# A graph block's last part: batch-normalised columns by graph or by node, and who issues the stores

## The reference

```python
x = layernorm(x + attention(x, bias=adj + adj))        # 16 heads, per graph
top1 = argmax(x.mean(nodes) @ router_w + router_b)      # one of 4 experts per graph
out = adj @ (x @ expert_w[top1])
mean, var = moments of out over all nodes of all graphs of the same expert, per feature
y = relu((out - mean[top1]) * rsqrt(var[top1] + eps) * gamma[top1] + beta[top1])
x = layernorm(x + y)
```

## Time and profile before

| what | us |
|---|---|
| runs: median (lowest to highest) | 3041.95 (3036.92 to 3044.52) |
| profiled execution, its own time | 3046.38 |
| its span, first to last instruction | 3044.6 |
| PE busy / DVE busy / ACT busy / POOL busy | 2802.0 / 2191.3 / 1772.6 / 750.3 |
| first instruction of `phase_two` on SP | 2713.8 |
| first scaling of the last part | 2735.4 |
| last final ends | 3039.94 |

### The profile page before, as it was taken

One profiled execution on the slowest core, in us unless ns is written; L12 is line 12 of the kernel. 1 busy time (PEld: TensorE's weight loads), 2 busy tenths in 40 slices (PEclk: granted clock), 3 DMA queues, 4 the chain that ended last, 5 costly groups with the idle time before them and its releaser, 6 DMA issues. The chain is left out here.

```text
span 3044.6 us, 70536 instructions
## 1 busy us (share of the span) xinstructions
PE 2802.0 (92%) x24130; PEld 2369.6 (78%) x24130; DVE 2191.3 (72%) x3938; ACT 1772.6 (58%) x6146; POOL 750.3 (25%) x431
## 2 busy tenths in 40 slices
PE   6899999999999999999999999999999999766675
PEld 6788888888888888888888888888888888655554
DVE  7777777777777777777777777777777777628776
ACT  3555655555565555556556555655655555517777
POOL 2022222222222222222222222222222222121111
PEclk9999999999999999999999999999999999867666
DMA  6344444444444444444444444444444444477887
GB/s 224 117 162 173 155 145 172 167 146 162 172 150 150 172 160 146 169 172 145 156 172 159 145 172 166 144 162 172 154 149 172 160 144 162 156 268 265 331 329 267
DMA packets 165115, 537.82 MB, mean 177 GB/s; under 512 B 15539, under 2 KB 48307, under 8 KB 122035
## 3 DMA queue, kind: packets, MB, share of 16 engines
q1 hardware_dynamic: 165042, 536.96, 49.4%
HBM read 427.84 MB, written 109.05 MB: 176 GB/s over the span
## 5 line engine op out<-in xcount | busy, mean ns | idle before, releaser
L548 ACT ACTIVATE prob<-prob,neg_max 128x128 f32<-128x128 f32 x2048 | 795.3, 394 | 361.9 <-DVE abs_max L675 361.9
L323 POOL TENSOR_TENSOR norm<-norm,constants 128x1 f32<-128x1 f32 x128 | 70.8, 553 | 1621.0 <-DVE norm L707 1621.0
L525 ACT ACTIVATE qk<-bank 128x512 f32<-128x512 f32 x256 | 153.1, 599 | 466.1 <-PE bank L343 466.1
L616 DVE SCALAR_TENSOR_TENSOR prob<-bank,adj_in 128x512 f32<-128x512 f32 x512 | 318.0, 684 | 137.0 <-PE bank L343 137.0
L548 ACT ACTIVATION_READ_ACCUMULATOR prob<-prob,neg_max 128x1 f32 x2048 | 394.1, 192 | 0.0
L334 POOL TENSOR_TENSOR moments<-moments,conv 128x1024 f32 x128 | 309.0, 2414 | 328.4 <-ACT conv L573 317.5
L633 DVE TENSOR_TENSOR prob<-prob,inv_sum 128x2048 f32<-128x2048 f32 x128 | 338.8, 2647 | 4.4
L343 PE MATMUL bank<-xT_hi,wq_hi 128*128 128x256 f32 x1024 | 303.4, 296 | 39.9 <-DVE wk_lo L587 19.1
L649 DVE TENSOR_REDUCE neg_max<-prob 128x16 f32<-128x2048 f32 x128 | 291.0, 2274 | 0.0
L343 PE MATMUL bank<-xT_hi,wq_lo 128*128 128x256 f32 x1024 | 290.1, 283 | 0.0
L343 PE MATMUL bank<-xT_lo,wq_hi 128*128 128x256 f32 x1024 | 290.1, 283 | 0.0
(11 more groups left out here) (111 smaller groups left out, 6465.2 us busy)
## 6 DMA issues: line engine op xcount, KB each, us to landing
expert_hi<-expert_hi_scratch SPq DMA_DIRECT2D x128, 1024.0 KB, 4.8
expert_lo<-expert_lo_scratch SPq DMA_DIRECT2D x128, 1024.0 KB, 7.5
xT_in<-xT SPq DMA_DIRECT2D x64, 512.0 KB, 8.5
x_in<-x SPq DMA_DIRECT2D x128, 256.0 KB, 7.9
x_scratch<-x SPq DMA_DIRECT2D x128, 256.0 KB, 8.3
conv_scratch<-conv SPq DMA_DIRECT2D x128, 256.0 KB, 8.4
conv_in<-conv_scratch SPq DMA_DIRECT2D x32, 1024.0 KB, 7.1
x_in<-x_scratch SPq DMA_DIRECT2D x32, 1024.0 KB, 9.1
```

The lines of the kernel that those rows point to most:

```text
L525: act.activation(qk[:, npar, c, :, :].rearrange("p k n -> p (k n)"), src[:, :], ACT.Copy).then_inc(qk_copied, 1)
L548: last = act.activation(prob[:, u % 2, h, :], prob[:, u % 2, h, :], ACT.Exp, bias=neg_max2[:, u % 2, h:h + 1], scale=2.0, accum_out=row_su ...
L616: dve.scalar_tensor_tensor(out=prob[:, u % 2, h:HEADS:HPC, :], in0=ps_heads[h][:, :].rearrange("p (c m) -> p c m", c=C), scalar=HALF_SCALE ...
```

## The change

The two scratch tensors are laid out (graph, node, feature). In the last part a partition holds four neighbouring nodes of one graph: partition b * 32 + i has nodes 4i to 4i + 3 of graph b of the group, so that loads and stores are contiguous runs of 8 KB on both sides, where the stores were four runs of 2 KB per partition. The slot's four rows (j) are now the four nodes of a partition. A turned 128 x 128 block therefore holds columns of all four graphs, in the order (b, i), and one feature chunk c of one j. PE gathers in a bank the four j of one chunk; a scaling instruction takes one chunk and one graph: four runs of 32 columns, 128 apart. ACT scales chunks 0, 1, 2, DVE chunk 3, so both need the experts of all four graphs of the group and read them at the head of the group. `bnT` gets two buffers of a whole group.

The step of the pipeline becomes one group instead of one graph, on PE, ACT and DVE. PE turns group g and then turns back g - 1; ACT scales g and finishes g - 2; DVE scales its chunk of g, makes the shift of g - 2 and joins g - 1. The store is issued by ACT, behind its four finals and a wait for them, and SP only loads, as soon as the slot's earlier store has landed.

```diff
-    x1_dram = nc.dram_tensor("x1_scratch", (P, B, D), F32, kind="Internal").ap()
+    x1_dram = nc.dram_tensor("x1_scratch", (B, N, D), F32, kind="Internal").ap()
...
-    conv_dram = nc.dram_tensor("conv_scratch", (P, B, D), F32, kind="Internal").ap()
+    conv_dram = nc.dram_tensor("conv_scratch", (B, N, D), F32, kind="Internal").ap()
...
+    def by_token(t, lo, n):
+        return t[bass.ds(lo, n), :, :].rearrange("b (i j) d -> (b i) (j d)", j=G)
+    def flat(t, r):
+        return t[:, r, :, :].rearrange("p j d -> p (j d)")
+    def per_graph(ps, b):
+        return ps[:, :].rearrange("p (j b i) -> p j b i", j=G, b=G)[:, :, b, :]
...
-                sp.dma_start(conv_in[:, r, :, :], conv_dram[:, bass.ds(g * G, G), :]).then_inc(ld_g[r], 16)
...
-            if live(g - STORE_LAG):
-                b, r2 = g - STORE_LAG, (r - STORE_LAG) % RING
-                sp.wait_ge(finished, (b + 1) * G)
-                sp.dma_start(out[bass.ds(b * G, G), :, :].rearrange("b n d -> n b d"),
-                             x1_in[:, r2, :, :]).then_inc(st_g[r2], 16)
+                sp.dma_start(flat(conv_in, r), by_token(conv_dram, g * G, G)).then_inc(ld_g[r], 16)
+                sp.dma_start(flat(x1_in, r), by_token(x1_dram, g * G, G)).then_inc(ld_g[r], 16)
```

On PE:

```diff
+        def group(k, r, live):
+            g = k * RING + r
+            if live(g):
+                pe.wait_ge(ld_g[r], (k + 1) * 32)
                 for c in range(C):
+                    if live(g - 1):
+                        if c < ACT_CHUNKS:
+                            pe.wait_ge(act_scaled, (g - 1) * ACT_CHUNKS + c + 1)
+                        else:
+                            pe.wait_ge(dve_scaled, (g - 1) * (C - ACT_CHUNKS) + c - ACT_CHUNKS + 1)
+                    for j in range(G):
+                        last = pe.transpose(ps_turned[c][:, j * P:(j + 1) * P],
+                                            conv_in[:, r, j, c * P:(c + 1) * P], ident[:, :])
+                    last.then_inc(turned, 1)
+            h = g - 1
+            if live(h):
+                pe.wait_ge(act_scaled, h * ACT_CHUNKS + ACT_CHUNKS)
+                pe.wait_ge(dve_scaled, h * (C - ACT_CHUNKS) + C - ACT_CHUNKS)
+                for j in range(G):
+                    if live(h - 1):
+                        pe.wait_ge(joined, (h - 1) * G + j + 1)
+                    for c in range(C):
+                        last = pe.transpose(ps_back[j][:, c * P:(c + 1) * P],
+                                            bnT[:, (r - 1) % 2, c, j, :, :].rearrange("p b i -> p (b i)"),
+                                            ident[:, :])
+                    last.then_inc(turned_back, 1)
```

On ACT:

```diff
+        def group(k, r, live):
+            g = k * RING + r
+            if live(g):
+                es = [act.value_load(expert_of[0:1, bass.ds(g * G + b, 1)], min_val=0, max_val=E - 1)
+                      for b in range(G)]
+                if live(g - 2):
+                    act.wait_ge(turned_back, (g - 1) * G)
+                for c in range(ACT_CHUNKS):
+                    act.wait_ge(turned, g * C + c + 1)
+                    for b in range(G):
+                        column = bass.ds(es[b] * C + c, 1)
+                        last = act.activation(bnT[:, r % 2, c, :, b, :], per_graph(ps_turned[c], b), ACT.Identity,
+                                              bias=shift_t[:, column], scale=scale_t[:, column])
+                    last.then_inc(act_scaled, 1)
+            h, r3 = g - 2, (r - 2) % RING
+            if live(h):
+                act.wait_ge(shift_made, h + 1)
+                for j in range(G):
+                    act.activation(x1_in[:, r3, j, :], x1_in[:, r3, j, :], ACT.Identity,
+                                   bias=shift[:, r3 % 4, j:j + 1],
+                                   scale=rstd[:, r3 % 4, j:j + 1]).then_inc(finished, 1)
+                act.wait_ge(finished, (h + 1) * G)
+                act.dma_start(by_token(out, h * G, G), flat(x1_in, r3)).then_inc(st_g[r3], 16)
```

On DVE:

```diff
+        def group(k, r, live):
+            g = k * RING + r
+            if live(g):
+                es = [dve.value_load(expert_of[0:1, bass.ds(g * G + b, 1)], min_val=0, max_val=E - 1)
+                      for b in range(G)]
+                if live(g - 2):
+                    dve.wait_ge(turned_back, (g - 1) * G)
+                for c in range(ACT_CHUNKS, C):
+                    dve.wait_ge(turned, g * C + c + 1)
+                    for b in range(G):
+                        column = bass.ds(es[b] * C + c, 1)
+                        last = dve.tensor_scalar(bnT[:, r % 2, c, :, b, :], per_graph(ps_turned[c], b),
+                                                 scale_t[:, column], shift_t[:, column], ALU.mult, ALU.add)
+                    last.then_inc(dve_scaled, 1)
+            if live(g - 2):
+                finish_stats(g - 2, (r - 2) % RING, live)
+            h, r1 = g - 1, (r - 1) % RING
+            if live(h):
+                join(h, r1, 0)
+                join(h, r1, 1)
+                take_stats(h, r1, 0)
+                join(h, r1, 2)
+                take_stats(h, r1, 1)
+                join(h, r1, 3)
+                take_stats(h, r1, 2)
+                take_stats(h, r1, 3)
+                dve.wait_ge(stats_taken, (h + 1) * G)
...
+                    last = dve.bn_aggr(mean_var[:, r1 % 2, j, :], stats[:, j, :])
...
```

More of the change, by code:

```diff
@@ L758, in phase_two @@
     x1_in = sb("x1_in", [P, RING, G, D])
-    bnT = sb("bnT", [P, G, C, P])
+    bnT = sb("bnT", [P, 2, C, G, G, ROWS])
     stats = sb("stats2", [P, G, 6])
@@ L787, in phase_two @@
     finished = sem("finished")
[L789 to L797, removed]
     def run_groups(eng, group, lag):
@@ L857, in _ @@
         pe.wait_ge(columns_ready, 1)
[L859 to L865, removed]
-                for c in range(C):
[L867 to L877, removed]
@@ L881, in _ @@
+        run_groups(pe, group, 1)
     @block.gpsimd
@@ L899, in _ @@
         act.wait_ge(columns_ready, 1)
[L901 to L918, removed]
@@ L922, in _ @@
+        run_groups(act, group, 2)
     @block.vector
@@ L964, in finish_stats @@
                                      in1=rstd[:, r % 4, :], op0=ALU.mult, op1=ALU.mult).then_inc(shift_made, 1)
[L966 to L984, removed]
-                dve.bn_stats(stats[:, j, :], x1_in[:, r, j, :]).then_inc(stats_taken, 1)
-                if j == G - 1:
-                    dve.wait_ge(stats_taken, m + 1)
-                    dve.sem_inc(dve_passed)
-                    for i in range(G):
-                        last = dve.bn_aggr(mean_var[:, r % 2, i, :], stats[:, i, :])
-                    last.then_inc(stats_joined, 1)
-                    dve.wait_ge(stats_joined, g + 1)
-                    dve.tensor_scalar(var_eps[:, r % 2, :], mean_var[:, r % 2, :, 1], EPS, None,
-                                      ALU.add).then_inc(var_ready, 1)
-            m, (r, j) = n - JOIN_LAG - 2, place(s, JOIN_LAG + 2)
-            if live(m) and j == G - 1:
-                finish_stats(k * RING + (s - JOIN_LAG - 2) // G, r, live)
@@ L999, in _, with join, take_stats @@
-        run_graphs(dve, graph, JOIN_LAG + 2)
+        def join(h, r, j):
+            dve.wait_ge(turned_back, h * G + j + 1)
+            dve.scalar_tensor_tensor(out=x1_in[:, r, j, :], in0=ps_back[j][:, :], scalar=0.0,
+                                     in1=x1_in[:, r, j, :], op0=ALU.max, op1=ALU.add).then_inc(joined, 1)
+        def take_stats(h, r, j):
+            dve.wait_ge(joined, h * G + j + 1)
+            dve.bn_stats(stats[:, j, :], x1_in[:, r, j, :]).then_inc(stats_taken, 1)
+        def group(k, r, live):
[25 more added lines that the diff above has]
+                dve.wait_ge(stats_taken, (h + 1) * G)
+                dve.sem_inc(dve_passed)
+                for j in range(G):
+                    last = dve.bn_aggr(mean_var[:, r1 % 2, j, :], stats[:, j, :])
+                last.then_inc(stats_joined, 1)
+                dve.wait_ge(stats_joined, h + 1)
+                dve.tensor_scalar(var_eps[:, r1 % 2, :], mean_var[:, r1 % 2, :, 1], EPS, None,
+                                  ALU.add).then_inc(var_ready, 1)
@@ L1002 @@
+        run_groups(dve, group, 2)
 def kernel(x, adj, L0_gnn_Wq, L0_gnn_Wk, L0_gnn_Wv, L0_gnn_Wo, L1_gnn_router_w, L1_gnn_router_b,
```

24 lines of the change are left out of this document (6 added, 18 removed).

## The result

The changed kernel takes 3107.23 us at the median of four runs (3106.27 to 3108.85), the kernel before 3040.76: ratio 1.0216, 95% interval 1.0204 to 1.0228. The forecast was 3070 in 3040 to 3102. The direction was right, the size was not: +66 us instead of +28. The profiled execution took 3108.85 us, its span 3107.0.

A forecast was written before the change was run, and what follows sets the result against it. The prediction took ACT's in-order queue to bound the last part: 10.2 us a group against 9.3, with fill, loops' ends and tail +27 to +28 us, added to the median 3041.95 for 3070 us, range 3040 to 3102.

The forecast's parts named there:

- What bounds the kernel before: Last part: ACT in order, 9.3 us a group, 7.08 of it work, 2.3 reads and waits for TensorE; transfers hidden.
- ACT, work: 12 scalings and 4 finals per group stay at 7.08 us; scalings in runs of 32 add 0.
- ACT, reads: Four expert reads at each group's head, none hidden, 0.6 us each, 2.4 in all; ends 0.38 and 1.0 a read.
- The rule of the Trainium skill: Floor near 600 ns for a tensor_load: four reads some 1.3 us dearer, stage about 40 us longer; set aside for 286 ns.
- ACT, store: Per group on ACT: wait for its own finals 0.03 us and store issue 0.6, ends 0.1 and 1.2.
- DVE 10.0 us, just under ACT: DVE's work and four reads per group sum to 10.0 us against ACT's 10.2, so it doesn't set the period.
- DMA: worth nothing: Stores going from 2 KB to 8 KB runs gain nothing, as a group asks for 308 GB/s, less than today's 333.
- Fill, loops, tail: Last part: round 3 starts at 25.3 us, three loops' ends add 4.7, the tail stays 16.4.
- The sum: Last part: last group's scaling starts 315.6 us after the first, against 288.2 before; total +27 to +28 us.
- Reads cheaper: Rival at each group's head: below 0.38 us a read the change wins, 3002 us with reads quite hidden; chance 0.08.
- ACT and DVE catch each other: Rival: both near 10 us a group, or short runs dearer, +0.8 a group, 3093 us; chance 0.16.
- The DMA rival: DMA engines are the real bound in the last part and 8 KB stores free them, 3010 us; chance 0.04.

The follow-up runs named there:

- b2: Kernel before, its store cut to the first 128 bytes of every row: 3015.85 us, ratio 0.9916 to the kernel before.
- e7: Changed kernel, its store cut to the first 512 bytes of every partition, order, waits and issues untouched: 3072.76 us, ratio 1.0101 to the kernel before.
- e2: Changed kernel with the store issued by SP again, four groups behind its loads; ACT neither waits nor issues: 3101.42 us, ratio 1.0191.
- e8: Changed kernel with the store on SP and the last part's loop written out, DVE's reads still at its group's head: 3087.80 us, ratio 1.0143.
- e6: Changed kernel with store on SP in 2 KB runs, no loop, ACT scaling all four chunks: 3014.63 us, beside 3013.21 us with 8 KB runs.
- e10: e4 with the wait for the finals and the store back on ACT: 3088.90 us, ratio 1.0151 to the kernel before.
- e3: Changed kernel with the three passes of the last part's loop written out, nothing else changed: 3090.35 us, ratio 1.0153 to the kernel before.
- e4: e8 with DVE reading the next group's experts one by one between its statistics and joins: 2988.34 us, ratio 0.9818 to the kernel before.
- e9: e4 with the store in four runs of 2 KB per partition, as in the kernel before: 2992.63 us, ratio 0.9833 to the kernel before.
- e1: Changed kernel with ACT's wait for finals and store issue moved behind its four expert reads: 3086.51 us, ratio 1.0140 to the kernel before.

## Why the prediction was wrong

The mechanism was right as far as it went: ACT's reads stand exposed behind its own wait and store, and ACT bounds the stage. The profile shows the signs that were named, one idle stretch a group put down to issue, scalings 0.34 apart, no wait for a load. The size of one term was not right, since two reads of a group are slowed by the store.

*What bounds the kernel before.* Right in naming ACT's in-order queue and in calling the transfers hidden. It took the 2.3 us of idle time for reads and waits for TensorE; b2 shows that about 0.9 of it was the collision.

*ACT, work: 7.08 us, runs of 32 at no charge.* Right: 7.10, scalings 0.34 apart.

*ACT, reads: four at 0.6, 2.4 us.* This is the step that failed. Measured 3.5: two of the four run beside the packets of the store that ACT has just issued, and are slow. The store and the reads were both in the sum, but priced one by one. The step had the warning in front of it, a load of 1683 ns, and put the end of its range at 1.0 us a read without asking which reads were long. Load by load, the trace of before shows it: from the fourth group on, the first and third read of a group take 0.27 to 0.30 us (one 0.37, and the first behind a branch 0.97 and 0.98), the second 0.65 to 1.71 in every group; the stores begin just there. The second read of the group of the earlier trace rows:

```profile
L907 ACTq TENSOR_LOAD <-expert_of x1: 1027/1027/1027, 2862.1 to 2862.1; - x1
```

By e7 against the changed kernel this is 35 of the 38 us that were missing. The range was also cut short of its own bound: reads at 1.0 us are 28 x 1.6 = 45 us, 3115, and it ended at 3102.

*The rule of the Trainium skill, a floor near 600 ns for a tensor_load (DMA: Bandwidth & Descriptors, "Latency and other measured facts").* The traces don't agree: the fastest loads of ACT take 0.27 us, and its median is 276 to 291 ns in every run. The rule's direction, four reads dearer than the sum had them, came true by another way, and that it came near in size (1.1 us a group, where an estimate by the rule gives 1.3) is chance.

*ACT, store: 0.63 us.* Near: from the end of the last final, 2890.44, to the first read's register operation it is 0.53.

*DVE 10.0 us, just under ACT.* Right where nothing collides: 9.9 in the last two groups of e8. It was the bound as soon as ACT was freed (e2, e8), with its own slow read 10.7 to 11.1.

*DMA: worth nothing.* Right at 8.3 us a group and above (e6). At 7.3, where the DMA engines are full, the longer runs are worth 4 us, which the intervals don't tell from none. The Trainium skill's row on HBM rows at a pitch of large powers of two (DMA: Bandwidth & Descriptors, the same section) had no bearing: its pitches begin at 512 KiB, and the 207 GB/s there is near the 214 that it calls full, so the forecast read it wrongly as slow. Here loads at 256 KB pitch and contiguous ones both reach 426 to 428 GB/s with the stores away.

*Fill, loops, tail.* Round 3 at 24.3 us, forecast 25.3. Loops: the forecast charged 1.57 us three times. There are two backward branches, and each costs more here, since ACT has no queued work to cover it: the two groups at a branch take 3.8 and 1.3 us over a normal one, although the reads behind the branch are spared the store. e3 prices all of the loop at 19 us. Tail 15.7, forecast 16.4.

*The sum.* First to last group's scaling: forecast 315.6, measured 351.7; with the small store 318.5. So with the slow reads out the forecast of the stage was 3 us off. That is partly luck: in e7 round 3 starts 2 us earlier than forecast, and the rest takes 5 us more.

*The rivals.* "Reads cheaper" needed 0.38 a read, they took 0.88. None of the rivals had a read that is slow beside a store. "ACT and DVE catch each other" isn't what happened in the changed kernel: ACT has no wait for DVE there, and e10 shows that ACT alone holds it at 11.0. The DMA rival became true only after both engines were freed.

## What to carry to other kernels

A wait on an in-order queue exposes everything behind it, so before moving a DMA issue to an engine list what its sequencer does next; here it was four register reads, which pass beside the finals when the wait is not there (e2). Moving the issue back alone showed 8 us, because another engine stood 0.2 us behind by the forecast's sums: two engines near the same period have to be freed together before either edit shows its worth (e8, e10 and e4: 1.014, 1.015 and 0.982). And when a small operation's row has a longest duration six times its median, look at which instances are long before using the median in a sum.

## What the runs showed of the hardware

- A TENSOR_LOAD of a register from SBUF takes 0.27 to 0.30 us on ACT and 0.30 to 0.33 on DVE, also beside loads that fill all DMA engines. When a 1 MB store is under way it can take 0.5 to 1.7 us: 54 of 81 of ACT's reads that overlap a store packet did in the changed kernel, 23 of 107 in e9. With the store cut to 64 KB all take 0.27 to 0.38 from 2780 us on (e7, b2). What it is in the store, its reading of SBUF or its writing of HBM, was not tried.
- Where the sequencer is ahead of its engine such loads cost the engine nothing, even between instructions that wait for semaphores (e4: 0.3 us of "issue" on DVE in 160 us).
- A backward branch can cost far more than the 1.57 us that stood in the chain. On ACT it is 4.7 us until the next register operation, before and after, and the work queued ahead of it covers what it can; in e1 and e2 it is 2.4 to 3.1. On DVE it was 0.3 us and is now 5.3, with 24 reads more in the loop; whether the longer loop is the cause wasn't tried. The branches of the loop, ACT's in the kernel before, then DVE's and ACT's in the changed one:

```profile
L793 ACTq COMPARE_BRANCH  x1: 54/54/54, 2874.9 to 2874.9; - x1
...
L793 ACTq FUSED_REGOPS  x1: 56/56/56, 2879.7 to 2879.7; - x1
```

```profile
L792 DVEq COMPARE_BRANCH  x1: 74/74/74, 2896.7 to 2896.7; - x1
L792 DVEq FUSED_REGOPS  x1: 92/92/92, 2902.1 to 2902.1; - x1
...
L792 ACTq COMPARE_BRANCH  x1: 54/54/54, 2902.4 to 2902.4; - x1
L792 ACTq FUSED_REGOPS  x1: 68/68/68, 2907.1 to 2907.1; - x1
```
